# Two layer-norm outputs moved from VectorE to TensorE: where ScalarE's seeds, the x products and the sums of the last stage stand

## The reference, cut to what matters

```python
x = _layernorm(x + _L0_attn_ref(x, ...))                 # x1 in the kernel
def step(c, xt):
    ft = sigmoid(xt @ wf.T + c @ uf.T + bf)
    it = sigmoid(xt @ wi.T + c @ ui.T + bi)
    gt = tanh(xt @ wc.T + c @ uc.T + bc)
    return ft * c + it * gt, None
c_final, _ = lax.scan(step, c0, x)
h = tanh(einsum('tbi,oi->tbo', x, wo) + c_final @ uo.T + bo)
return _layernorm(x + h)
```

## Time and profile before

| | us |
|---|---|
| median of 3 runs (lowest to highest) | 99.59 (99.39 to 99.7) |
| the profiled execution | 99.58 |
| its span in the trace | 97.8 |
| PE busy | 87.8 (90%) |
| DVE busy | 83.1 (85%) |
| ACT busy | 69.3 (71%) |
| POOL busy | 37.1 (38%) |

### The profile page before, as it was taken

How to read it: one execution, slowest core, us unless ns; L and a number is a source line. 1 busy time by engine, 2 the same in 40 slices (tenths; PEclk the granted TensorE clock), 3 DMA queues, 4 the chain that set the end, 5 groups by cost and what they waited for, 6 DMA issues and landing times.

```text
span 97.8 us, 1943 instructions
## 1 busy us (share of the span) xinstructions
PE 87.8 (90%) x606; PEld 77.9 (80%) x606; DVE 83.1 (85%) x248; ACT 69.3 (71%) x145; POOL 37.1 (38%) x54
## 2 busy tenths in 40 slices
PE   5987999999999999999999999999999999998000
PEld 4757879889688988988899989999999999895000
DVE  4495499999999998899889989999767897999970
ACT  0656977869798697788869445679495777999460
POOL 3006268003292094068019703440320413555750
PEclk9999999999999999999999999999999999999955
DMA  1899996000000000000000000000000003023636
GB/s 47 228 369 370 400 389 239 7 3 0 0 0 0 3 7 0 0 0 0 0 0 0 0 7 3 3 0 0 7 0 0 0 0 114 24 87 107 215 107 215
DMA packets 5378, 7.21 MB, mean 74 GB/s; under 512 B 500, under 2 KB 3320, under 8 KB 5368
## 3 DMA queue, kind: packets, MB, share of 16 engines
q1 hardware_dynamic: 4792, 6.69, 19.4%
q10 hardware_dynamic: 576, 0.40, 1.6%
HBM read 4.99 MB, written 2.10 MB: 72 GB/s over the span
## 4 chain that ended last, share of the span: by engine, by line
PE 70%; DVE 17%; issue 3%; ACT 3%; DMA 3%; POOL 1%; DVEq 0%; SPq 0%; ACTq 0%
PE ps_ctx L490 7%; PE ps_ctx L510 6%; DVE stats L1264 4%; DVE x L1283 4%; PE ps_k L428 4%; PE ps_x L524 4%; PE ps_q L479 4%; DMA row<-rows 3%; DVE x L1253 2%; PE ps_ctx L500 2%; PE ps_f L547 2%; PE ps_ctx L501 2%; PE ps_f L556 2%; PE ps_c L547 1%; PE ps_c L549 1%
## 5 line engine op out<-in xcount | busy, mean ns | idle before, releaser
L338 POOL TENSOR_TENSOR k_pair<-k_rows 128x256 f32<-128x256 f32 x8 | 5.9, 740 | 25.4 <-DVE s L1118 17.1
L347 POOL TENSOR_TENSOR rstd<-var_eps,minus_half 128x4 f32<-128x4 f32 x8 | 8.3, 1034 | 8.1 <-DVE var_eps L1057 7.6
L367 POOL TENSOR_TENSOR rstd<-var_eps,minus_half 128x4 f32<-128x4 f32 (+1 forms) x9 | 8.8, 987 | 3.5 <-DVE var_eps L1271 3.3
L374 POOL TENSOR_TENSOR s_lo<-s,s_hi 128x512 fp32r<-128x512 f32 (+1 forms) x6 | 6.6, 1106 | 8.4 <-ACT s_hi L835 8.4
L1066 DVE TENSOR_SCALAR x<-x,stats,rstd 128x128 f32<-128x128 f32 x28 | 9.0, 383 | 0.0
L490 PEld LDWEIGHTS ps_ctx<-k_rows,x_rows 128*128 128x128 f32 x56 | 7.1, 191 | 2.0 <-issue 1.8
L490 PE MATMUL ps_ctx<-k_rows,x_rows 128*128 128x128 f32 x56 | 7.5, 277 | 1.0 <-DVE k_rows L1093 0.8
L895 ACT ACTIVATE x_hi<-ps_x 128x512 fp32r<-128x512 f32 x8 | 4.8, 602 | 5.0 <-PE ps_x L524 5.0
L1081 DVE SCALAR_TENSOR_TENSOR x<-ps_ctx,z_inv,x_rows 128x128 f32<-128x128 f32 x28 | 8.0, 341 | 0.1
L1111 DVE SCALAR_TENSOR_TENSOR new<-th_i,th_c 128x256 f32<-128x256 f32 (+1 forms) x12 | 6.1, 512 | 2.1 <-ACT th_c L819 1.9
L510 PEld LDWEIGHTS ps_ctx<-kvo,q_cols 128*128 128x128 f32 x56 | 7.2, 191 | 0.8 <-issue 0.5
(11 more groups left out here) (242 smaller groups left out, 295.4 us busy)
## 6 DMA issues: line engine op xcount, KB each, us to landing
x_rows<-x SPq DMA_DIRECT2D x8, 256.0 KB, 6.0
x_cols<-xt SPq DMA_DIRECT2D x7, 256.0 KB, 5.9
out<-x SPq DMA_DIRECT2D x7, 256.0 KB, 2.2
wgate<-w_gate SPq DMA_DIRECT2D x1, 384.0 KB, 4.5
out<-x SPq DMA_DIRECT2D x2, 128.0 KB, 2.0
x_cols<-xt SPq DMA_DIRECT2D x1, 128.0 KB, 2.5
x_cols<-xt ACTq DMA_DIRECT2D x1, 128.0 KB, 2.4
wvo_in<-w_vo_in ACTq DMA_DIRECT2D x1, 128.0 KB, 3.5
```

Of the source, the lines that this page charges most:

```text
L338: nc.gpsimd.tensor_tensor(k_pair[:], k_rows[:, a % 2, 0:C // 2], k_rows[:, a % 2, C // 2:C], ALU.add).then_inc(k_pair_ok, 1)
L347: nc.gpsimd.tensor_tensor(rstd[:, b], var_eps[:, b], minus_half[:], ALU.pow).then_inc(rstd_ok, 1)
L367: nc.gpsimd.tensor_tensor(part_of(rstd, u, T), part_of(var_eps, u, T), minus_half[:, 0:nt * H].rearrange("p (t c) -> p t c", c=H), ALU.pow ...
L374: nc.gpsimd.tensor_tensor(s_lo[:, t % 2, part], state(t)[:, part], s_hi[:, t % 2, part].bitcast(F32), ALU.subtract).then_inc(slo_ok[k], 1)
```

## The change

- Units 1 to 3 join `PRELOADED`: ScalarE copies g into their banks (`preload`), and `g_high`, `g_low`, `add_g` and the rounded identity `ident_r` are gone.
- Unit 5 leaves `PRELOADED` and joins `DIRECT`: its state product is made by four matmuls of its own, behind `out_s(4)`.
- The x product of unit 4 stands where that of unit 1 stood, behind piece 9's gates and ahead of the last two states, and that of unit 5 stands behind that of unit 3, ahead of the last state.
- Units 4 and 5 join `IN_PSUM`: TensorE adds x1 to them, and VectorE's residuals 4 and 5 are gone.
- The banks of the units, the shares of normalisation and the order of the tail on VectorE and ScalarE change with it.

```diff
-DVE_NORM = [1, 1, 2, 2, 2, 3, 0, 2, 2]
-IN_PSUM = (6, 7, 8)
+DVE_NORM = [2, 2, 2, 3, 0, 0, 4, 0, 2]
+IN_PSUM = (4, 5, 6, 7, 8)
...
-DIRECT = (0, 4)
-PRELOADED = (5, 6, 7, 8)
+DIRECT = (0, 4, 5)
+PRELOADED = (1, 2, 3, 6, 7, 8)
...
-        unit_bank = [ps_q[:], ps_f[:], ps_c[:], ps_x1[:], ps_q[:], ps_f[:], ps_c[:], ps_ctx[:, 0, H * D:],
+        unit_bank = [ps_q[:], ps_x1[:], ps_q[:], ps_x1[:], ps_f[:], ps_c[:], ps_q[:], ps_ctx[:, 0, H * D:],
...
-                    mm = nc.tensor.transpose(ps_x1[:, c * D:(c + 1) * D], x1[:, b, c], ident[:])
+                    mm = nc.tensor.matmul(ps_x1[:, c * D:(c + 1) * D], x1[:, b, c], ident[:], start=(c == 0),
+                                          stop=(c == C - 1), is_transpose=True, skip_group_check=True)
...
             gates_s(9)
-            out_x(1)
+            out_x(4)
+            out_bias(4)
             out_s(0)
             out_g(0)
...
-            add_g(1)
+            out_x(1)
             out_x(2)
-            add_g(2)
             gates_x(11)
             gates_s(11)
             out_x(3)
-            add_g(3)
-            out_x(4)
+            out_x(5)
+            out_bias(5)
             out_g(1)
             out_s(4)
-            out_x(5)
+            out_s(5)
+            add_x1(4)
             out_x(6)
+            add_x1(5)
             out_x(7)
             out_x(8)
             add_x1(6)
...
             def preload(u):
 
                 nt = UNITS[u][1]
-                act.wait_ge(g_mm, 2)
-                if u == 5:
-                    act.wait_ge(w_ok, 2)
-                if u == 6:
-                    act.wait_ge(w_ok, 3)
+                act.wait_ge(g_mm, 1 if UNITS[u][2] == 0 else 2)
+                if u in (2, 3, 6):
+                    act.wait_ge(w_ok, {2: 1, 3: 2, 6: 3}[u])
...
-            act.wait_ge(ident_ok, 1)
-            nc.scalar.activation(ident_r[:], ident[:], ACT.Copy).then_inc(ident_r_ok, 1)
...
             second_residual(0)
             state_low(9)
-            g_low()
             second_statistics(0)
...
-            second_residual(4)
             second_statistics(4)
...
+            second_statistics(6)
+            second_variance(6)
+            second_shift(5)
+            second_statistics(7)
+            second_variance(7)
+            second_statistics(8)
+            second_variance(8)
+            second_normalise(6, 0, 2)
+            second_shift(7)
+            second_normalise(6, 2, 4)
+            second_normalise(8)
```

More of the change, by code:

```diff
@@ L217, in build @@
         g_pre_ok = sem("g_pre_ok")
[L218 removed]
+        g_mm = sem("g_mm")
         block = ctx.enter_context(nc.Block())
@@ L297, in act_norms, with shifts @@
             return sum(len(blocks(u)) - DVE_NORM[u] for u in range(units))
+        def shifts(u):
+            return sum(DVE_NORM[v] < len(blocks(v)) for v in range(u + 1))
         @block.sync
@@ L600, in out_x @@
                     pe.wait_ge(y_small_ok, T)
-                if u == 1:
+                if u == 4:
                     pe.wait_ge(f_ok, first_done)
-                if u == 2:
+                if u == 5:
                     pe.wait_ge(c_ok, first_done)
-                if u == 4:
-                    pe.wait_ge(w_ok, 1)
-                pe.wait_ge(x1c_ok, T if u >= 3 else UNITS[u][0] + UNITS[u][1])
+                pe.wait_ge(x1c_ok, UNITS[u][0] + UNITS[u][1])
                 if u in PRELOADED:
@@ L615, in out_x @@
                     mm.then_inc(out_mm, 1)
[L616 to L619, removed]
             def out_bias(u):
@@ L640, in out_g @@
             def out_g(h):
-                ps = g_bank[h]
+                ps = g_bank
                 if h == 0:
@@ L653, in out_g @@
                                  start=False, stop=True, skip_group_check=True).then_inc(g_mm, 1)
[L655 to L665, removed]
             def add_x1(u):
@@ L969, in _ @@
             state_high(9)
-            g_high()
+            preload(1)
+            preload(2)
             gates_tanh(10)
@@ L974, in _ @@
             out_tanh(2)
+            preload(3)
+            gates_tanh(11)
             normalise(0)
-            gates_tanh(11)
             out_tanh(3)
-            normalise(1)
-            preload(5)
-            out_tanh(4)
             preload(6)
-            out_tanh(5)
             preload(7)
             preload(8)
+            out_tanh(4)
+            normalise(1)
+            out_tanh(5)
+            normalise(2)
             out_tanh(6)
-            normalise(2)
             out_tanh(7)
@@ L991, in _ @@
             normalise(5)
-            normalise(6)
+            normalise(7)
         @block.vector
@@ L1278, in second_shift, with second_normalise @@
                                                part_of(rstd, u, T), ALU.mult, ALU.mult).then_inc(shift_ok, 1)
-            def second_normalise(u):
+            def second_normalise(u, j0=0, j1=None):
                 dve.wait_ge(rstd_ok, T + u + 1)
-                for t, c in blocks(u)[:DVE_NORM[u]]:
+                for t, c in blocks(u)[j0:DVE_NORM[u] if j1 is None else j1]:
                     nc.vector.tensor_scalar(x1[:, t, c], sum_of(u)[:, t - UNITS[u][0], c - UNITS[u][2]], mean_of(T + t, c),
@@ L1301, in _ @@
             second_statistics(2)
-            second_normalise(1)
+            second_normalise(0)
             second_residual(3)
@@ L1312, in _ @@
             second_normalise(3)
[L1313 to L1321, removed]
+            second_statistics(5)
+            second_variance(5)
+            second_shift(4)
+            second_normalise(4)
+            second_statistics(6)
[9 more added lines that the diff above has]
+            second_normalise(8)
 def kernel(**inputs):
```

19 lines of the change are left out of this document (5 added, 14 removed).

## The result

The changed kernel took 98.87 us (median of 6 runs, 98.61 to 99.11); the kernel before took 99.53 (6 runs, 99.35 to 99.93). The ratio is 0.9927, with a 95% interval of 0.9901 to 0.9952: faster by 0.7%, 0.66 us. A second measurement, beside experiments 10 to 12, gave 98.79 against 99.54, ratio 0.9940 (0.9919 to 0.9960). 99.0 had been foretold.

The account below looks back on a forecast made before the run. VectorE was taken to bound the end from 82.6 us. With TensorE then the bound, statistics at 90.32, a 3.54 tail and 0.06 put unit 6's DMA at 93.92, unit 8's at 94.90; span 97.24 + 1.78 = 99.0, range 98.5 to 99.7.

Parts of the forecast that it names:

- The bound moves from VectorE to TensorE: Last stage: TensorE becomes the bound until about 90 us, and VectorE waits some 0.8 before unit 6's statistics.
- Pieces 10 and 11: Last two states: piece 10's tanh moves from 76.31 to 76.54, piece 11's starts about 80.45, `out_x(3)` at 80.94.
- From g to unit 6's statistics: TensorE from 80.94 on: second g, ScalarE's copies, x products alternating with additions; unit 6's statistics start at 90.32.
- the 0.19: Ahead of the addition of x1 to unit 4: TensorE waits 0.19 for unit 4's tanh, which ends at 85.49.
- the wait of 0.3: VectorE was to stand idle for 0.3 before unit 4's statistics, waiting for TensorE.
- The tail: From unit 6's statistics: variance, root, four normalisations, 3.54 in sum, and 0.06 more to unit 6's DMA at 93.92.
- The last link: SyncE issues units 6, 7 and 8 at 0.49 each; from unit 8's issue the span goes on for 2.34.
- that rival: ScalarE ends last with units 4 and 5's normalisations: no change, 99.6; chance 0.23, shared with part of the dearer alternation.
- The dearer alternation: Rival: five TensorE groups from `add_x1(4)` to `add_x1(6)` take 0.2 more each, end at 100.0; chance of slower 0.12.

Follow-up runs that it names:

- experiment 10: The changed kernel with unit 8's x product behind unit 6's addition of x1, run again beside the changed kernel on one chip: 98.51 us, ratio 0.9903.
- experiment 11: The kernel before with only x1 of units 4 and 5 added by TensorE, normalisation shares fitted to it: 100.48 us, ratio 1.0100.
- experiment 12: The changed kernel with unit 7's output DMA issued by ScalarE and unit 5's output DMA left out: 98.81 us, ratio 0.9939.
- experiment 3: The changed kernel with three of unit 6's four x products left out, so its output is not the layer's: 98.16 us, ratio 0.9872.
- experiment 6: The changed kernel with unit 8's x product behind unit 6's addition of x1 and its tanh inside unit 4's normalisations: 98.49 us, ratio 0.9904.
- Experiment 4: The changed kernel with g for units 1 to 3 again added by TensorE from two rounded halves: 100.05 us, ratio 1.0066.
- experiment 8: The changed kernel with VectorE's three SBUF normalisations of unit 3 moved behind unit 6's variance, beside GpSimd's root: 99.47 us, ratio 1.0002.
- Experiment 2: The changed kernel with unit 6 normalised by ScalarE and unit 7 by VectorE, as before the change: 99.25 us, ratio 0.9989.
- experiment 5: The changed kernel with unit 7's output DMA issued by ScalarE instead of SyncE: 98.75 us, ratio 0.9922.
- experiment 1: The changed kernel with x1 added to units 4 and 5 by VectorE again instead of TensorE: 99.80 us, ratio 1.0037.

## Why the prediction was right

- **The bound moves from VectorE to TensorE.** Right, and the core of it. The chain is on TensorE to 90.1, VectorE waits 0.79 before unit 6's statistics (0.8 foretold), and experiments 3 and 6 show that less TensorE work, or the same work in another order, alone moves the end. (In the kernel before, the chain was not VectorE's to its very end, as I had it: GpSimd's root for unit 7 stands in it at 92.89 with 0.71.)
- **Pieces 10 and 11.** Right to a few hundredths: tanh of piece 10 at 76.51 (76.54), that of piece 11 at 80.44, released by TensorE (80.45), the x product behind it at 80.95 (80.94). The two copies of g ahead of piece 10's tanh cost nothing. Experiment 4 shows what the copies are worth on TensorE.
- **From g to unit 6's statistics.** 90.17 for 90.32. ScalarE's three copies took 1.02 until the next start instead of 1.13, so unit 4's tanh came at 84.76 instead of 84.91 and TensorE did not wait the 0.19 for it. An x product that leads into an addition lasts 0.89 to 0.90 like any other, not 0.96. The 0.96 came from a row in the kernel before in which TensorE had just been released by ScalarE. Against these two stands the first addition with 0.96 until the x product behind it, for 0.87. So 90.17 is closer to the forecast than its terms were: they erred both ways. One sign failed: the wait of 0.3 that VectorE was to show before unit 4's statistics was not there. The sum was there at 85.42 + 1.13 = 86.55, and VectorE came free at about the same moment and started at 86.58.
- **The tail.** 3.58 from the statistics to unit 6's DMA, for 3.60. The root took 1.01, as chosen between 1.01 and 1.10, and experiment 8 shows that VectorE's operation under way at its start decides it. Whether this saved time is not shown: the root ended at 92.22, VectorE's last variance just then (92.11 + 0.17), and the first normalisation started at 92.26. Experiment 2 shows that taking the new shares back costs 0.5.
- **The last link.** Wrong in its reason, and right in its number by luck. I had unit 8's issue as the last thing, 0.49 for each issue and 2.34 behind it. Experiments 5 and 12 show that an earlier issue gains nothing, and the windows show why: the transfer of the last 512 KB starts with unit 6 and runs without a gap. Since both kernels issue the three in the same way, 0.98 + 2.34 = 3.32 held in both.
- **ScalarE** ended unit 5 at 92.79 (92.95) and had 0.96 to spare. Experiments 1 and 2 show how near that rival was: with the residuals or unit 6's blocks back in their old place it ends last.
- The dearer alternation did not happen: of the five groups, four took 0.86 to 0.90 and one 0.96.

The gain is 0.66 by the medians (0.75 in the second measurement), for 0.56 foretold in the span. The span fell to 97.1, where 97.24 was foretold; that is the 0.15 that I had too much on TensorE. The parts do not add up to the gain: each of experiments 1, 2 and 4 takes back more or nearly as much as the whole change gave, because each part opens room that another uses. No run took back the new places of the x products of units 4 and 5 or unit 5's own state product, so what those are worth is not shown.

## What to carry to other kernels

When work goes from one full engine to another, the gain is decided by what else is taken off the receiver and by what then stands in front of the last waits: here the additions with shares to fit them made the kernel 1.0% slower, and with the copies on ScalarE, the new places and the new tail it became 0.7% faster. Walk the receiving engine row by row to the last point where another waits for it, and put nothing in front of that point that is needed only later; moving unit 8's x product behind it gave another 0.3 us or so for nothing. At the very end, count the bytes of the last outputs and when the first of them is issued, before shortening the issue of the last.

## What the runs showed of the hardware

- The last three output transfers, 512 KB, ran at 343 GB/s with the DMA engines full (experiment 12, 95 to 96 us), and the span's end stayed 3.3 to 3.4 us behind the first one's issue when the last one's issue came 0.36 us earlier.
- GpSimd's power operation on 128x4 took 1.01 us beside VectorE operations from PSUM or none (unit 0's took 1.04 in the kernel before). It took 1.05 to 1.26 where a VectorE operation from SBUF to SBUF was under way at its start: 1.05 when that one had begun 0.17 us before, 1.10 or 1.11 at 0.10. Further ones that began while it ran added nothing.
- Where TensorE waited for ScalarE's tanh before an addition of x1, its weight load waited too: in experiment 1 the load starts at 87.54 and the pass at 87.55, behind waits of 0.85 and 0.66. The group of four rows then lasts 1.13 and not 1.03.
- Profiles of kernels that are alike up to 70 us do not stand at the same times there: at 7 us the rows stood 0.3 us earlier in one and 0.8 us later in another, as much as the whole change, and one that stood level at 7 us was 0.2 earlier at 86 us (experiment 5).
